# An attention and feed-forward layer on one core: another order of loads, splits and jobs in the first half-block

## The reference, cut to what matters

```
xn = layernorm(x)                                  # over the 512 features
q, k, v = split(xn @ local_qkv_w)                  # 512 -> 3 x 128, full softmax attention
local   = softmax(q @ k.T * scale) @ v
q, k, v = split(xn @ sparse_qkv_w)                 # the same, but only the top 102 of 1024 scores
sparse  = softmax(where(s >= kth, s, -1e9)) @ v
xp  = xn @ memory_proj_w                           # memory head: 64 slots of 128
mem = concat(xp, softmax(xp @ bank.T) @ bank) @ mem_out_w + mem_out_b
h   = xn @ pred_in_w + pred_in_b                   # prediction head
pred = gelu(h @ pred1_w + pred1_b) @ pred2_w + pred2_b
s = concat(local, sparse, mem, pred) @ warboss_w + warboss_b
g = silu(relu(xn @ w1 + b1) @ w2 + b2)             # 512 -> 2048 -> 512
out = x + s * g
```

## Time and profile before

| | |
|---|---|
| three runs | 2586.85, 2587.35, 2587.92 us; median 2587.35 |
| profiled execution, its own time | 2589.47 us |
| its span in the trace | 2587.7 us |
| TensorE matmul busy | 2535.0 us (98%) |
| VectorE busy | 2317.5 us (90%) |
| ScalarE busy | 1363.0 us (53%) |
| GpSimd busy | 1118.1 us (43%) |
| mean granted TensorE clock | 0.993 of full speed |

### The profile page before, as it was taken

The page is one execution under the profiler, slowest core; times in us unless marked ns, Lnnn a source line. Parts: engine busy times, 40 slices in busy tenths (PEclk is TensorE's granted clock), DMA queues, the critical chain, the costliest instruction groups (busy, mean ns, idle before and its releaser), DMA issues.

```text
span 2587.7 us, 37027 instructions
## 1 busy us (share of the span) xinstructions
PE 2535.0 (98%) x12900; PEld 2149.0 (83%) x12900; DVE 2317.5 (90%) x5194; ACT 1363.0 (53%) x2311; POOL 1118.1 (43%) x862
## 2 busy tenths in 40 slices
PE   6999999889999999999999999999999999999998
PEld 5888888778888888888888888888888888888886
DVE  7666666589999999999999999999999999999996
ACT  5777777634444444444444444444445454444443
POOL 4445554423444444444444444444444444444444
PEclk9999999989999999999999999999999999999999
DMA  6887788774566456645664566456645654565454
GB/s 217 302 306 296 294 311 305 294 267 155 196 213 217 163 196 214 214 166 196 216 215 164 196 215 214 165 197 215 214 164 196 213 210 163 196 230 200 165 201 166
DMA packets 166776, 558.60 MB, mean 216 GB/s; under 512 B 18048, under 2 KB 31040, under 8 KB 158144
## 3 DMA queue, kind: packets, MB, share of 16 engines
q1 hardware_dynamic: 166592, 556.24, 60.9%
HBM read 421.96 MB, written 134.22 MB: 215 GB/s over the span
## 4 chain that ended last, share of the span: by engine, by line
PE 94%; DVE 4%; DMA 1%; POOL 1%; ACT 0%; issue 0%; POOLq 0%; SPq 0%; ACTq 0%
PE acc L59 9%; PE acc L61 9%; PE acc L60 9%; PE hid L61 9%; PE hid L59 9%; PE hid L60 9%; PE ps L59 5%; PE ps L61 5%; PE ps L60 5%; PE o L59 5%; PE o L61 5%; PE o L60 5%; PE scores L1299 4%; PE scores L59 2%; PE scores L61 2%; PE scores L60 2%
## 5 line engine op out<-in xcount | busy, mean ns | idle before, releaser
L1052 POOL TENSOR_TENSOR h_lo<-h,h_hi 128x512 fp32r<-128x512 f32 x256 | 333.7, 1304 | 866.6 <-ACT h_hi L950 865.4
L1192 DVE MAX8 top_l<-larger 128x8 f32<-128x512 f32 x832 | 576.4, 693 | 13.2
L1212 DVE MATCH_REPLACE8 larger<-top_l,larger 128x512 f32<-128x512 f32 x768 | 521.6, 679 | 0.0
L949 ACT ACTIVATE h<-hid,small 128x512 f32<-128x512 f32 x256 | 176.5, 690 | 483.3 <-PE hid L61 483.3
L59 PE MATMUL acc<-w2s,h_hi 128*128 128x512 f32 x1024 | 412.1, 402 | 0.0
L59 PE MATMUL hid<-xnT,w 128*128 128x512 f32 x1024 | 400.3, 391 | 4.4 <-DMA w<-ffn_scratch 4.4
L61 PE MATMUL hid<-xnT,w 128*128 128x512 f32 x1024 | 400.5, 391 | 0.0
L61 PE MATMUL acc<-w2s,h_lo 128*128 128x512 f32 x1024 | 400.3, 391 | 0.0
L60 PE MATMUL acc<-w2s,h_hi 128*128 128x512 f32 x1024 | 400.2, 391 | 0.0
L60 PE MATMUL hid<-xnT,w 128*128 128x512 f32 x1024 | 400.0, 391 | 0.0
L1052 POOL TENSOR_TENSOR pT_s<-pT,pT_s 128x512 fp32r<-128x512 f32 x256 | 326.7, 1299 | 52.5 <-ACT pT_s L962 52.5
(11 more groups left out here) (175 smaller groups left out, 5593.5 us busy)
## 6 DMA issues: line engine op xcount, KB each, us to landing
w2s<-ffn_scratch SPq DMA_DIRECT2D x259, 512.0 KB, 3.9
w<-ffn_scratch SPq DMA_DIRECT2D x258, 512.0 KB, 4.2
tl<-tile_scratch SPq DMA_DIRECT2D x66, 512.0 KB, 3.9
xnT_scratch<-xnT SPq DMA_DIRECT2D x16, 2048.0 KB, 13.6
kv_scratch<-kv_out SPq DMA_DIRECT2D x32, 1024.0 KB, 5.6
tile_scratch<-tiles_out SPq DMA_DIRECT2D x16, 2048.0 KB, 8.3
xnT<-xnT_scratch SPq DMA_DIRECT2D x64, 512.0 KB, 7.0
xin<-in_L_attn_x SPq DMA_DIRECT2D x17, 1024.0 KB, 9.1
```

The source lines that it names most:

```text
L949: nc.scalar.activation(h32[:, c % 2, :], hid[:, :], ACT.Relu, bias=bias)
L1052: return nc.gpsimd.tensor_tensor(out_, value, hi_.bitcast(F32), ALU.subtract).then_inc(ready, 1)
L1192: l_step = count(nc.vector.max(top_l[:, own], larger[:, :]))
L1212: l_step = count(nc.vector.match_replace(larger[:, :], top_l[:, own], larger[:, :], LOWEST))
```

## The change

It changes the prologue and half 0 of stage 1. Nothing is computed differently.

- Half 0 of `xin` comes in four loads with a semaphore each. The load of the second half's tokens stands before the two rows and `ww`, no longer behind them.
- ScalarE makes the high parts of the `mp` and `pi` weights first, in one instruction, then the others in four. VectorE makes their low parts (`w_first`) behind `layer_norm(0)`.
- GpSimd starts on the other weights' low parts only when the first half's transposed tokens are split (`xlo_ready` 4): five instructions, by projection. The low parts of `ww` follow, counted by `ww_split`.
- ScalarE makes `ww_hi` behind job `qs` of half 0, no longer before the first job. The `wait` of `kl` is for `ww_split`.
- VectorE calls `layer_norm(1)` behind the memory weights (`wn_ready`) of half 0, no longer before `steps`. The split of the small weights stands behind that of the tokens.
- Half 0 has its own order `FIRST_JOBS`, and the bank product stands behind `pi`.

```
+FIRST_JOBS = ["mp", "pi", "ql", "ms", "p1a", "p1b", "qs", "kl", "ks", "v01", "wt", "tr0", "p2", "tr1", "mo", "tr2",
+              "tr3", "v23"]
...
             def _(sp):
-                sp.dma_start(xin[:, :, :], x[0, 0:HALF, :].rearrange("(t p) d -> p t d", p=P)).then_inc(x_in, 16)
+                for t in range(HTILES):
+                    sp.dma_start(xin[:, t, :], x[0, t * P:(t + 1) * P, :]).then_inc(x0_in[t], 16)
...
+                sp.wait_ge(xn_ready, 1)
+                sp.dma_start(xin[:, :, :], x[0, HALF:S, :].rearrange("(t p) d -> p t d", p=P)).then_inc(x_in, 16)
                 sp.dma_start(b2[:, :], w["b2"].partition_broadcast(P)).then_inc(rows_in, 16)
...
-                for k in range(2 * KT):
-                    pool.wait_ge(w_h, k + 1)
...
+                pool.wait_ge(xlo_ready, KT)
+                pool.wait_ge(w_h, 1 + KT)
+                for m, size in ((QL, 1), (QS, 1), (KL, 1), (KS, 1), (VL, 2)):
+                    c = slice(m * P, (m + size) * P)
+                    pool.tensor_tensor(wp_lo[:, :, c], wp[:, :, c], wp_hi[:, :, c].bitcast(F32), ALU.subtract)\
+                        .then_inc(w_split, 1)
+                for k in range(KT):
+                    pool.wait_ge(w_h, 2 + KT + k)
+                    pool.tensor_tensor(ww_lo[:, k, :], ww[:, k, :], ww_hi[:, k, :].bitcast(F32), ALU.subtract)\
+                        .then_inc(ww_split, 1)
...
                 act.wait_ge(mp_in, 32)
+                nc.scalar.activation(wp_hi[:, :, 0:2 * P], wp[:, :, 0:2 * P], ACT.Copy).then_inc(w_h, 1)
...
-                act.wait_ge(ww_in, 16)
-                for k in range(KT):
-                    nc.scalar.activation(ww_hi[:, k, :], ww[:, k, :], ACT.Copy).then_inc(w_h, 1)
...
-                                        act.wait_ge(w_split, KT)
+                                        act.wait_ge(w_first, 1)
+                                        act.wait_ge(w_split, 5)
...
-                                        act.wait_ge(w_split, 2 * KT)
+                                        act.wait_ge(ww_split, KT)
...
+                            if (n, name) == (0, "qs"):
+                                act.wait_ge(ww_in, 16)
+                                for k in range(KT):
+                                    nc.scalar.activation(ww_hi[:, k, :], ww[:, k, :], ACT.Copy).then_inc(w_h, 1)
...
+                dve.wait_ge(w_h, 1)
+                subtract(wp_lo[:, :, 0:2 * P], wp[:, :, 0:2 * P], wp_hi[:, :, 0:2 * P]).then_inc(w_first, 1)
...
-                layer_norm(1)
...
                         nc.vector.tensor_copy(we[:, :, 0, :], we[:, :, 1, :]).then_inc(wn_ready, 1)
+                        if first(n):
+                            layer_norm(1)
```

More of the change, by code:

```diff
@@ L54, with jobs @@
 T_QL, T_QS, T_MEM, T_PRED = range(4)
+def jobs(n):
+    return FIRST_JOBS if n == 0 else JOBS
 def product(nc, out, w_hi, w_lo, x_hi, x_lo, first, last):
@@ L113, in stage1 @@
     LAST = 2 * B - 1
+    ORDER = [(n, name) for n in range(2 * B) for name in jobs(n)]
+    PLACE = {job: KT + i for i, job in enumerate(ORDER)}
     XP, PIN, WT = range(3)
@@ L185, in stage1 @@
         x_in = sem("x_in")
+        x0_in = [sem(f"x0_in{t}") for t in range(HTILES)]
+        w_first = sem("w_first")
+        ww_split = sem("ww_split")
         ln_step = sem("ln_step")
@@ L351, in steps @@
                         n = 2 * b + hh
-                        for name, slot in (("ql", T_QL), ("qs", T_QS), ("kl", "kl"), ("ks", "ks"), ("p2", T_PRED),
-                                           ("mo", T_MEM), ("v01", 0), ("v23", 1)):
+                        slots = {"ql": T_QL, "qs": T_QS, "kl": "kl", "ks": "ks", "p2": T_PRED, "mo": T_MEM,
+                                 "v01": 0, "v23": 1}
+                        for name in (name for name in jobs(n) if name in slots):
+                            slot = slots[name]
                             if n == LAST and name == "v23":
@@ L403, in steps @@
                         n = 2 * b + hh
-                        for name in JOBS:
+                        for name in jobs(n):
                             src = ps[:, bank(n, name), :]
@@ L487, in layer_norm @@
                         nc.vector.sem_clear(ln_step)
-                    dve.wait_ge(x_in, 16 * (n + 1))
+                    if not first(n):
+                        dve.wait_ge(x_in, 16 * n)
                     step = [0]
@@ L517, in _ @@
                 layer_norm(0)
+                dve.wait_ge(w_h, 1)
+                subtract(wp_lo[:, :, 0:2 * P], wp[:, :, 0:2 * P], wp_hi[:, :, 0:2 * P]).then_inc(w_first, 1)
+                for k in range(KT):
+                    dve.wait_ge(bank_read, k + 1)
+                    subtract(xnT[:, 0, k, LOW, :], xnT32[:, k, :], xnT[:, 0, k, HI, :])\
+                        .then_inc(xlo_ready, 1)
                 dve.wait_ge(sm_in, 16 * SM_LOADS)
@@ L544, in steps @@
                             subtract(act_lo[:, slot, :], act32[:, slot, :], act_hi[:, slot, :]).then_inc(lo_ready, 1)
+                        if first(n):
+                            dve.wait_ge(bm_out, 1)
+                            subtract(bm_lo[:, :], bm[:, :], bm_hi[:, :]).then_inc(bm_split, 1)
                         dve.wait_ge(job_done, done(n, "ms"))
@@ L574, in steps @@
                             subtract(xnT[:, 1 - hh, k, LOW, :], xnT32[:, k, :], xnT[:, 1 - hh, k, HI, :]).then_inc(xlo_ready, 1)
+                        if first(n):
+                            dve.wait_ge(rows_in, 16 * 2)
+                            nc.vector.tensor_scalar(half_bias[:, :], half_bias[:, :], 0.5, None, ALU.mult)
                         if n < LAST:
@@ L624, in steps @@
                                 c = slice(columns[name] * P, (columns[name] + 1) * P)
+                                if first(n) and name in ("ql", "qs", "kl", "ks"):
+                                    pe.wait_ge(w_split, ("ql", "qs", "kl", "ks").index(name) + 1)
                                 for k in range(KT):
@@ L672, in steps @@
                                 v = slice(VL * P, (VS + 1) * P)
+                                if first(n):
+                                    pe.wait_ge(w_split, 5)
                                 for tt in range(2):
```

35 lines of the change are left out of this document (12 added, 23 removed).

## The result

The changed kernel takes 2595.19 us, the median of nine runs (2593.97 to 2596.14). The kernel before takes 2587.35 us in the runs beside it. The ratio is 1.003, with a 95% interval of 1.002 to 1.004: slower by 0.3%. The profiled execution took 2596.14 us with a span of 2594.5 us.

A forecast was written before the change was run, and what follows sets the result against it. TensorE was taken to bound stage 1 once it runs. Half 1 starting 5.9 us later plus 0.2 us within it gave +6.1; the forecast was 2587.35 + 6.0 = 2593.3 us, range 2583.0 to 2596.0.

The forecast's parts named there:

- its likeliest case: Whole kernel: the late, held second norm outweighs the early start, giving 2592 to 2595 us; chance 0.48.
- its case "worse": Rival: full clock cost of 3.05 us, `sm_in` at 18.4 and late stores give +8, 2595.5 us; chance 0.10.
- Its +6.1: Whole kernel: half 1 starting 5.9 us later, plus 0.2 us lost within half 1, on a span of 2587.7 us.
- the 6.0 in its last step: Final addition to the earlier kernel's median: 2587.35 + 6.0 = 2593.3 us.
- First norm and `sm_in`: Start of half 0: `xn` ends at 11.95, copies wait for small loads until 17.75, `mp` starts 7.35 us earlier.
- Two starts at the same moment: Half 0, behind `ms`: the second norm's chain of twelve and GpSimd's `ww_lo` both start at 38.2 us.
- One VectorE operation per GpSimd instruction: Second norm: ten GpSimd instructions (13.7 us) hold it; `xn` ready at 54.2, TensorE waits 10.3 us before `tr0`.
- Two-input operations: Second norm's chain: small two-input operations L508 and L509 are held by GpSimd too, as the skill's rule says.
- the rival that lets them slip through: Second norm: L508 and L509 aren't held, `xn` ready about 52.2, total +4.1 us, 2591.4 us; chance 0.22.
- The clock: TensorE from `p2` to half 1: lower clock after the long wait costs 2.0 us, between 0 and 3.05.
- Half 1 onward: Half 1: later norm and low part of `mp` cost 0.2 us (0 to 1); late stores are hidden, costing nothing.

The follow-up runs named there:

- Run 4: Changed kernel with ScalarE's wait for the small loads and the bank's transpose moved behind `mp`, so the first copies don't wait for them: 2592.75 us.
- Run 2: Changed kernel with GpSimd's four low parts of `ww` (128x512) made in sixteen instructions of 128x128: 2589.75 us.
- run 5: Changed kernel with ScalarE making `ww_hi` behind job `pi` instead of behind `qs`: 2590.19 us.
- run 1: Changed kernel with the call of `layer_norm(1)` moved from behind the memory weights to behind the maxima of the memory scores: 2591.5 us.
- Run 6: Changed kernel with the store of the transposed tokens put ahead of the next token load in SyncE's queue: 2593.37 us.
- Run 3: Changed kernel with the second norm's call, `ww_hi` and the job order put back where the kernel before has them: 2592.8 us.
- run 9: Changed kernel with `ww_lo` in sixteen instructions, copies before small loads, token store before load, norm behind the maxima, and raw `ww` in the values' slots: 2587.2 us.
- run 7: Changed kernel with `ww_lo` in sixteen instructions, first copies not behind the small loads, and the transposed tokens' store ahead of the token load: 2587.4 us.

## Why the prediction was right

It named 2593.3 us (2583.0 to 2596.0) and slower as the likeliest; 2595.19 was measured. That is 7.8 us slower where 6.0 was named, 0.2 above the upper edge of its likeliest case (2592 to 2595) and near its case "worse" (2595.5). The mechanism was right and the sum a little short. Its +6.1 gives 2593.45; the 6.0 in its last step is a slip of 0.1. On the spans of the profiled executions, for which the +6.1 was worked out, the change is 6.8. The other 1.0 us is that the profiled execution lies 2.1 us above the median before and 0.95 above it after, which no step can be charged with. Its steps, against the trace after:

- **First norm and `sm_in`.** `xn` through at 12.30 (11.95 named), the copies at 17.30 (17.75), `mp` at 19.25 (19.6). Run 4 confirms the gate. I counted three more issues of 0.47 us ahead of the small loads; the last of them is issued at 14.05, only 0.25 later. The four parts of `xin` take 1.8 us of issue in place of 0.44, but the eight weight loads behind them take 6.2 in place of 7.2.
- **Two starts at the same moment.** Both named at 38.2, both found at 38.71. Part of that is luck: TensorE was through `ms` 0.56 us earlier than named, and from there the memory weights took 1.2 us longer. On the way one thing was not in my sum: `bm_lo` is held 2.47 us by GpSimd's splits, so the memory scores, ready for VectorE at about 30.3, are read at 31.70. The five splits took 9.49 us, not the 7.4 to 8.5, and end at 31.6.
- **One VectorE operation per GpSimd instruction.** Ten instructions in 13.5 us (13.7 named), `xn` ready at 54.33 (54.2), a wait of 11.09 (10.3) because TensorE reached tr0 at 43.4. Run 2 changes only the length of GpSimd's instructions beside the norm, run 5 their number (by an earlier place on ScalarE), and the wait follows both. The lock is shown, not argued.
- **Two-input operations.** L530 and L531, the L508 and L509 of before, took 1.18 to 1.21 us each, so the rival that lets them slip through is out (the first of the list, though the prediction calls it the second in one place). The rule of the Trainium skill, page "SBUF — State Buffer", section "Who interferes with whom", by which a VectorE instruction with two SBUF inputs and a GpSimd instruction that reads SBUF shut each other out for their whole length, agrees with the trace here: 1.2 us for an operation that takes 0.16. The one-input L526 and L528 on four elements were held just as long, 1.15 and 1.21 us, and in run 1 so were the `we` of 64 elements.
- **The clock.** From `p2` at 56.34 to half 1 it is 9.08 us, where the work at full speed takes 7.1: the 2.0 us that I took between 0 and 3.05. The matmuls show the lower level until about 60.6 us.
- **Half 1 onward.** This is the term that was mis-sized, and the reason for its main part was wrong. I took 0.2 us for the later norm and low part of `mp`, and nothing for the stores, which I called hidden, since half 1 needs them 8 us on. The norm and the low part cost 0.34 us. The stores cost the rest of the 1.29 us of half 1, 0.95. I had the order of the queue right but not what a pile-up does to a landing: 12.71 us against the 8 us that I had room for. Run 6 takes the pile-up away and gets these 0.95 back.

Where the early start went: at `ms` (29.48 in place of 37.89) it is 8.41 us. The waits before tr0 and `p2` take 11.09 and 0.77, and the rest from tr0 on 10.17 in place of 7.47 (59.33 less 48.93, less 2.93 for `v01`, which now stands ahead), 2.70 for the lower clock. That makes the 6.09 at half 1, within 0.1. Run 3 shows that the norm's old place doesn't avoid the row either.

One thing stays open: nothing here tells why the later halves take 29.51 us in some runs and 29.53 in others.

## What to carry to other kernels

When work of GpSimd is moved off one stretch of VectorE, look for the VectorE operations that it lands beside and count instructions on both sides, not bytes: here ten GpSimd instructions in a row held ten VectorE operations, however small. If it must run beside a chain of small dependent operations, cut its instructions shorter before reordering anything. And a load that waits for a late result doesn't only come late itself: it keeps back every store queued behind it. Last, when one engine's wait is gone, look for the next one: run 9 gained 1.7 us in half 0 and lost 1.5 of it in half 1, to VectorE.

## What was not expected of the hardware

- The hold goes both ways, where the prediction read from rows 3 and 4 that GpSimd loses nothing. Five splits (four of 128x512, one of 128x1024) took 9.49 us beside VectorE's subtractions, where single ones of that kind take 1.25 and 2.39, 7.4 together. GpSimd's sixteen instructions of 128x128 took 7.45 us beside the chain and `xn`, and 8.75 beside `xn`, the memory weights and the gelu split.
- The lower clock came after short waits too. In run 7, after a wait of 2.86 us, the granted clock was 0.50 of full speed from 43.4 to 50 us; in the changed kernel, after the wait of 11.09 us, it was 0.51 from 54.4 to 60.6. A matmul of 512 columns took 0.77 us at the start of `p2` in both. Over 20 us of run 7 the mean was 0.74:

```profile
40.00:60.00 20.00, 13.61 (x63) 0.74 0.49 182
```
